# Graph layers on one core: GpSimd waits for each group of four gathers to land before it issues the next

## What is computed

```python
alpha = leaky(a_src[src] + a_dst[dst])        # or a dot product of q[dst] and k[src]
a = exp(alpha - segment_max(alpha, dst)[dst])
out = segment_sum(h[src] * a / segment_sum(a, dst)[dst], dst)
```

## Time and profile before

| | |
|---|---|
| median of three timed runs | 3976.72 us (3972.66 to 3978.0) |
| profiled execution, span | 4992.2 us |
| mean granted TensorE clock in it | 0.776 |
| busy share of the span, PE / DVE / ACT / POOL | 68% / 62% / 35% / 53% |
| gathers, all passes | 2346, of 0.95 us each on POOL |
| DMA traffic | 554.64 MB, 111 GB/s in the mean |

### The profile page before, as it was taken

How to read it: one execution, slowest core, us unless ns; L and a number is a source line. 1 busy time by engine, 2 the same in 40 slices (tenths; PEclk the granted TensorE clock), 3 DMA queues, 4 the chain that set the end, 5 groups by cost and what they waited for, 6 DMA issues and landing times. The chain is left out here.

```text
span 4992.2 us, 80536 instructions
## 1 busy us (share of the span) xinstructions
PE 3385.8 (68%) x15489; PEld 2315.7 (46%) x15489; DVE 3110.9 (62%) x10883; ACT 1739.5 (35%) x5661; POOL 2633.7 (53%) x2962
## 2 busy tenths in 40 slices
PE   6366665666677467777777778556666666666999
PEld 4244443444445344444444445334444444433998
DVE  6355555655567555666666667656666666667886
ACT  3333333333335444545455555311121221121332
POOL 3555555555540345555555543555555555553787
PEclk8666677776769788888888889767777777677999
DMA  4444444444433433333333334534433333332221
GB/s 144 134 127 122 125 121 122 127 123 126 122 97 90 129 94 105 107 106 107 103 108 108 110 86 150 182 106 112 112 108 110 111 108 108 109 107 81 72 73 53
DMA packets 286529, 554.64 MB, mean 111 GB/s; under 512 B 83599, under 2 KB 180941, under 8 KB 286126
## 3 DMA queue, kind: packets, MB, share of 16 engines
q0 software_dynamic: 115872, 326.30, 23.8%
q10 hardware_dynamic: 97688, 160.93, 10.6%
q1 hardware_dynamic: 72566, 63.01, 4.5%
HBM read 473.68 MB, written 76.32 MB: 110 GB/s over the span
## 5 line engine op out<-in xcount | busy, mean ns | idle before, releaser
L483 PE MATMUL psum<-big,onehots_or_distances 128*128 128x264 f32 (+2 forms) x4992 | 2151.6, 541 | 1058.1 <-DVE acc L654 486.6
L483 PEld LDWEIGHTS psum<-big,onehots_or_distances 128*128 128x128 f32 x4992 | 1025.5, 250 | 1419.8 <-issue 1274.7
L654 DVE TENSOR_TENSOR acc<-acc,psum 128x264 f32 (+2 forms) x2496 | 1046.1, 419 | 773.7 <-DMA acc<-in_edges_dram,acc 237.2
L267 POOL DMA_INDIRECT big<-table_attn,src_by_edge x782 | 739.8, 946 | 764.5 <-SPq L260 352.2
L267 POOL DMA_INDIRECT big<-table_typed,src_by_edge x782 | 740.3, 947 | 618.7 <-SPq L260 380.8
L267 POOL DMA_INDIRECT big<-table_gat,src_by_edge x782 | 739.2, 945 | 608.5 <-SPq L260 379.1
L373 ACT ACTIVATE onehots_or_distances<-psum 128x512 f32<-128x512 f32 x416 | 248.1, 596 | 1665.6 <-DMA joins<-visit_joins 524.3
L632 DVE TENSOR_TENSOR big<-big,psum 128x256 f32<-128x256 f32 x1664 | 669.1, 407 | 91.6 <-issue 58.7
L426 PE MATMUL psum<-big,onehot_t 128*128 x2496 | 490.5, 311 | 228.7 <-issue 138.8
L508 DVE SCALAR_TENSOR_TENSOR dot_products<-psum,big 128x258 f32<-128x258 f32 x832 | 348.1, 419 | 449.0 <-PE psum L426 228.0
L344 ACT ACTIVATE onehots_or_distances<-iota,tables 128x128 f32<-128x128 f32 x832 | 330.3, 397 | 669.1 <-DVE acc L654 428.5
(11 more groups left out here) (280 smaller groups left out, 4192.3 us busy)
## 6 DMA issues: line engine op xcount, KB each, us to landing
onehot_t<-onehots ACTq DMA_DIRECT2D x68, 512.0 KB
big<-visit_positions ACTq DMA_DIRECT2D x52, 512.0 KB
onehots<-big ACTq DMA_DIRECT2D x36, 512.0 KB
big<-onehots ACTq DMA_DIRECT2D x36, 512.0 KB
big<-in_x_dram SPq DMA_DIRECT2D x98, 128.0 KB, 2.8
big<-table_gat,src_by_edge POOLq DMA_INDIRECT x782
big<-table_attn,src_by_edge POOLq DMA_INDIRECT x782
big<-table_typed,src_by_edge POOLq DMA_INDIRECT x782
```

The lines of the kernel that those rows point to most:

```text
L267: pool.indirect_dma_start(X[:, t % RING, :], None, ph.table, bass.IndirectOffsetOnAxis(ap=m.src[:, t:t + 1], axis=0)).then_inc(S[f"rows{t ...
L483: nc.tensor.matmul(sum_ps(v), onehot_at(v), rows, start=True, stop=True).then_inc(S["summed"], 1)
L654: nc.vector.tensor_tensor(row, row, sum_ps(v), ALU.add).then_inc(S["added"], 1)
```

## The change

In each edge pass, in front of each group of four gathers but the first, POOL also waits until all four gathers of the group that it has just issued have landed. The wait is on that group's semaphore, at 64 increments for each turn of the ring so far. It stands behind the wait for ring room.

```diff
             for t in range(NT):
                 if t >= RING and t % QUARTER == 0:
                     pool.wait_ge(S["freed"], t // QUARTER - groups + 1)
+                if t >= QUARTER and t % QUARTER == 0:
+                    q = t // QUARTER - 1
+                    pool.wait_ge(S[f"rows{q % groups}"], 16 * QUARTER * (q // groups + 1))
                 pool.indirect_dma_start(X[:, t % RING, :], None, ph.table,
                                         bass.IndirectOffsetOnAxis(ap=m.src[:, t:t + 1], axis=0)).then_inc(S[f"rows{t // QUARTER % groups}"], 16)
```

## The result

The changed kernel takes 5450.1 us (median of three, 5446.34 to 5452.94) against 3976.72 us: a ratio of 1.371, 95% interval 1.369 to 1.374. It is slower by 1473 us. The forecast was slower by 833 us, with the landings that are waited for as the cause; 5450 lies outside its range of 4250 to 5050.

A forecast was written before the change was run, and what follows sets the result against it. The prediction took the chain over DVE, PE and ACT to bound the profiled passes, with gathers nearly the bound when timed. With the change, 588 groups x 6.6 = 3881 us plus 930 for the rest gave 4810 us, range 4250 to 5050.

The forecast's parts named there:

- The step from the profile to the timed runs: Edge passes, timed: gathers still 1.25 us each, passes 3047 us, 5.2 a group against 5.0 needed, cover 0.2 us.
- The rest of the program: Node phases, filling of a pass and its end: 930 us in the timed runs, ends 850 and 1000.
- Step (b): Wait before each group: landing takes 1.9 us (1.8 to 2.4) instead of 0.30, so a group takes 6.6 us.
- (a): The 585 added wait instructions on POOL: 10 us at 17 ns each, bounded by 0 and 59; taken as 0.
- the runs of twelve: POOL in the passes: twelve gathers in a row at 1.25 us, catching up after a ring wait; forecast to vanish.
- The sign that ScalarE and PE wait far more than 61.6 and 3.0 us: Edge passes: waits for SyncE's report of arrival would grow far beyond 61.6 us (ScalarE) and 3.0 us (PE).
- The forecast of the profiled span: Whole changed kernel under the profiler: near 5050 us, growing 0 to 6%, while the timed median grows by a fifth.
- 1 (the issue is cheaper in timed runs): Between gathers: 0.05 instead of 0.30 us without the profiler, group 5.85 us, total 4370 (4230 to 4600); chance 0.17.
- 2: Whole kernel: gather, landing and demand all shrink by 0.797, only lost catching up costs, 81 us, total 4058; chance 0.12.
- 3: Group starts on POOL: the ring wait already covers the new wait, so time stays 3977 us; chance 0.03.
- 4 (faster): DMA engines: spaced gathers let ACT's loads arrive sooner, 24 us less in timed terms, 3953 us; chance 0.04.
- The estimate from the Trainium skill: Gather landing: about 2.0 us fixed plus bytes over 436 GB/s, 2.3 us for 133 KB, group 7.0, total about 5050.

The follow-up runs named there:

- second profile of the kernel before: The unchanged kernel timed and profiled once more, nothing changed against the kernel before: 3972.4 us, profiled span 3971.9 us.

## Why the prediction was wrong in size

- **The step from the profile to the timed runs held.** It said that gathers cost 1.25 us there too, that the other engines' stops were not in them, and that a group takes about 5.2 us with a cover of 0.2. The second profile of the kernel before has 1.25 us, no such stops, 5.05 us a group and a cover of 0.05. The rest of the program was taken as 930 us and is 974.6 in the changed kernel; this is 45 us more.
- **Step (b), with (a), failed in size: the distance between groups was put at 1.9 us and is 2.89 in the mean.** Over 588 groups it is (7.61 - 6.60) x 588 = 594 us. With the 45 that makes 639 of the 640 us that were missed. Its parts, from the trace of the changed kernel and the runs:
  - The landing, from a last gather's end to SyncE's report, is 1.86 us in the median, as predicted, and 2.17 in the mean: some 160 us. The prediction had 4.4 us in one of five sampled rows and a mean of 2.4, and took the common value. In a serial chain the mean counts. It expected the late ones to grow few with fewer groups queued; those beside ScalarE's transfers stayed, and 109 us came off when the two large transfers in gat were parted.
  - The way from the landing to the next gather was set to nothing, POOL's start being taken equal to SyncE's report. Where the wait rides in the gather it is 0.24 us: some 140 us.
  - Where the wait stands alone the gather starts another 0.5 us later, at the 555 steady places: some 280 us, and the swapped order takes off 314. The prediction priced the instruction at nothing "since the wait that it makes covers it", with an upper end of 59 us. That end came from the instruction's own 17 ns; it left out the way from the wait to the gather, for which the trace of before had no row.
  - The 27 late second gathers are 30 us. The four parts sum to 610; the ends of the passes, where there is no wait, take off most of the difference to 594.
- **Mechanism and place were right.** The gathers became the bound, no group start has less than 2.0 us in front of it, the runs of twelve are gone, the consumers wait for arrival. Halving the waits halves the loss; waiting for a landing two groups back costs 13 us. The sign that ScalarE and PE wait far more than 61.6 and 3.0 us was set against the disturbed profile; the second has 424 and 49.
- **The forecast of the profiled span (near 5050, 0 to 6% over 4992) was wrong:** 5448.5, 9% over. It took the stops of that one execution as part of every profile, and took 1.9 us between groups as in the main sum.
- **Rivals.** 1 (the issue is cheaper in timed runs) falls: the second profile of the kernel before has 0.30 us between its gathers, and the time of that execution, 3973.9 us, lies among the timed ones beside it (3964.8 to 3975.5). 2 and 3 (all shrinks alike, no effect) and 4 (faster) fall: late large transfers do exist, but parting them is worth 14 us in the kernel before.
- **The Trainium skill.** The estimate from the Trainium skill (DMA: Bandwidth & Descriptors, "Anatomy of one DMA — SWDGE (gpsimd) path"), 2.3 us and 5050 in total, was nearer in total than my 4810, but it prices the landing alone. The trace of the changed kernel has 1.86 us in the median and 2.17 in the mean for that, and most of what is missing is the way from the landing to the next gather.

## What to carry to other kernels

A wait for one's own last transfer puts its whole landing, the way back to the next issue and every late case into each turn; price it by the mean of many rows, not by the common one, and look whether the slack that seems to cover it exists in an execution as long as the timed ones. If a profile's span and the timed median differ by more than a per cent, take it again before any share is read from it. Where two waits stand in front of a gather on POOL, put the one that is met last first in the program, or fold both into one; on other engines this was not tried.

## What was not expected of the hardware

- Of two waits in front of a gather on POOL, the one written last becomes an instruction of its own. If that one blocks, the gather starts 0.74 us after it passes; if the other blocks, riding in the gather, the gather starts 0.24 us after the landing is reported, and the stand-alone wait has passed a group earlier. Over three passes this is 314 us.
- Two 512 KB transfers issued 0.4 us apart lengthened the distance of the group beside them to 5.1 us in the mean of 51, where the median of all is 2.61; the same bytes apart made it 2.8 to 3.0.
- One execution of an unchanged program was 26% longer than its second profiled one (4992.2 against 3971.9 us), at the same cost of each gather, while sequencers of other engines stood: instructions that take 33 ns at most in the second profile took up to 1396 ns.
